# Cross-attention over 12,544 keys: values per tile, one matmul per head with high and low parts side by side, denominators on DVE, elementwise work in tiles of 1024 columns

## The reference

```python
lat = layernorm(latents, ln_l_w, ln_l_b)
ctx = layernorm(context, ln_c_w, ln_c_b)
q = (lat @ Wq).reshape(b, n, H, D).transpose(0, 2, 1, 3)
kv = ctx @ Wkv
k, v = jnp.split(kv, 2, axis=-1)
...
attn = jnp.einsum('bhnd,bhsd->bhns', q, k) * scale
attn = jnp.clip(attn, -11.0, 11.0)
attn = jax.nn.softmax(attn, axis=-1)
out = jnp.einsum('bhns,bhsd->bhnd', attn, v)
out = out.transpose(0, 2, 1, 3).reshape(b, n, INNER)
return out @ Wo + bo
```

## Time and profile before

| | us |
|---|---|
| median of three runs | 1161.74 (1159.35 to 1161.77) |
| profiled execution, its own time | 1157.79 |
| its span, first to last instruction | 1156.1 |
| PE busy | 1137.3 (98%) |
| DVE busy | 829.5 (72%) |
| ACT busy | 598.8 (52%) |
| POOL busy | 309.0 (27%) |

### The profile page before, as it was taken

How to read it: one execution, slowest core, us unless ns; L and a number is a source line. 1 busy time by engine, 2 the same in 40 slices (tenths; PEclk the granted TensorE clock), 3 DMA queues, 4 the chain that set the end, 5 groups by cost and what they waited for, 6 DMA issues and landing times.

```text
span 1156.1 us, 18331 instructions
## 1 busy us (share of the span) xinstructions
PE 1137.3 (98%) x5056; PEld 936.4 (81%) x5056; DVE 829.5 (72%) x1622; ACT 598.8 (52%) x1029; POOL 309.0 (27%) x516
## 2 busy tenths in 40 slices
PE   6999999999999999999999999999999999999997
PEld 5888888888888888888888888888888888888774
DVE  5778778777777777787776776776766766766624
ACT  4555555555555555555555555555555555555411
POOL 5334334334334233242221221221211211211100
PEclk8999999999999999999999999999999999999996
DMA  5221221221211211354212212212112112110000
GB/s 178 69 69 46 68 68 45 68 63 51 68 61 53 68 55 59 108 108 81 74 46 69 67 46 68 62 51 68 57 56 68 53 61 68 51 64 24 1 1 5
DMA packets 81393, 70.72 MB, mean 61 GB/s; under 512 B 40115, under 2 KB 67670, under 8 KB 81366
## 3 DMA queue, kind: packets, MB, share of 16 engines
q1 hardware_dynamic: 80390, 68.94, 20.1%
q10 hardware_dynamic: 976, 1.45, 0.4%
HBM read 70.13 MB, written 0.13 MB: 61 GB/s over the span
## 4 chain that ended last, share of the span: by engine, by line
PE 96%; issue 2%; DMA 1%; DVE 1%; POOL 0%; ACT 0%; SPq 0%; POOLq 0%; DVEq 0%; ACTq 0%
PE bank L466 31%; PE bank L467 31%; PE bank L468 31%; PE bank L511 1%; DMA wkT<-in_WkT_dram 1%; PE bank L572 1%; PE bank L584 1%; PE bank L503 0%; PE bank L614 0%; PE bank L596 0%; PE bank L630 0%; PE bank L594 0%; POOL wkT L457 0%; DVE fold_y L909 0%; PE bank L604 0%
## 5 line engine op out<-in xcount | busy, mean ns | idle before, releaser
L732 ACT ACTIVATE ex<-bank,c_rstd 128x512 f32<-128x512 f32 x392 | 270.1, 689 | 242.4 <-PE bank L468 166.4
L403 POOL TENSOR_TENSOR z_lo<-z,z_hi 128x255 fp32r<-128x255 f32 x196 | 174.9, 892 | 742.1 <-ACT z_hi L745 742.1
L739 ACT CAST p_hi<-ex 128x512 fp32r<-128x512 f32 x392 | 243.8, 622 | 240.8 <-DVE ex L899 148.6
L903 DVE TENSOR_TENSOR p_lo<-ex,p_hi 128x512 fp32r<-128x512 f32 x392 | 271.6, 693 | 116.3 <-ACT p_hi L739 99.7
L466 PE MATMUL bank<-qk_hi,d_hi 128*128 128x512 f32 x784 | 305.9, 390 | 0.0
L467 PE MATMUL bank<-qk_lo,d_hi 128*128 128x512 f32 x784 | 305.5, 390 | 0.0
L466 PE MATMUL bank<-p_hi,z_hi 128*128 128x512 f32 x784 | 305.5, 390 | 0.0
L468 PE MATMUL bank<-p_hi,z_lo 128*128 128x512 f32 x784 | 305.5, 390 | 0.0
L468 PE MATMUL bank<-qk_hi,d_lo 128*128 128x512 f32 x784 | 305.3, 389 | 0.0
L467 PE MATMUL bank<-p_lo,z_hi 128*128 128x512 f32 x784 | 305.2, 389 | 0.0
L899 DVE TENSOR_SCALAR ex<-ex 128x512 f32<-128x512 f32 x392 | 189.8, 484 | 156.5 <-ACT ex L732 154.6
(11 more groups left out here) (162 smaller groups left out, 410.0 us busy)
## 6 DMA issues: line engine op xcount, KB each, us to landing
t_all<-in_ctxT_dram SPq DMA_DIRECT2D x98, 384.0 KB, 3.2
x_pair<-in_ctx_dram SPq DMA_DIRECT2D x98, 256.0 KB, 2.7
diff<-sig_all SPq DMA_DIRECT2D x194, 0.5 KB, 1.9
wq<-in_Wq_dram ACTq DMA_DIRECT2D x2, 512.0 KB, 6.9
wkT<-in_WkT_dram SPq DMA_DIRECT2D x2, 512.0 KB, 6.1
wv<-in_Wv_dram SPq DMA_DIRECT2D x1, 1024.0 KB
wo<-in_Wo_dram SPq DMA_DIRECT2D x1, 1024.0 KB
crow_all<-in_crows_dram ACTq DMA_DIRECT2D x1, 256.0 KB, 7.6
```

The source lines that it names most:

```text
L403: pool.tensor_tensor(z_lo[s][:, b, 0:LAST], z[s][:, b, 0:LAST], z_hi[s][:, b, 0:LAST].bitcast(F32), ALU.subtract).then_inc(s_zlo, 1)
L732: act.activation(ex[c][:, :], sc_bank[c][:, :], ACT.Exp, scale=c_rstd[s4][:, b:b + 1])\
L739: act.copy(p_hi[b][c][:, :], ex[c][:, :]).then_inc(s_phi, 1)
L903: dve.tensor_tensor(p_lo[b][c][:, :], ex[c][:, :], p_hi[b][c][:, :].bitcast(F32), ALU.subtract)\
```

## The change

Three things change in the main loop. First, the values are made per tile: `values` multiplies the tile (`d_hi`, `d_lo`) with folded value weights `wv_hi`, `wv_lo` into one bank (128 keys x 512, 8 heads of 64), ACT and DVE split it into `vhl`, where each head's 64 high and 64 low columns lie side by side; z is gone, and with it POOL's part. Second, `weighted_sum` is one matmul per head: stationary `[v_hi | v_lo]` (128 columns), moving `[p_hi | p_lo]` of that head (256 columns). The four products land in four quarters of the result; the lo·lo one is summed too. `save_part` and `save` add the column halves; the halves on the partitions are added by a product with Wo stored twice (`wo2`). Third, the denominators are summed by DVE (`add_den`, 1024 columns per tile), added over the partitions by a matmul with ones, inverted 512 columns at a time (`inverse`) and multiplied in (`normalised`). The exponential stays in chunks of 512; clip, `p_hi` and `p_lo` take 1024 columns.

Around the loop: the weight folds for keys and values are matmuls with `foldT` (before the loop for pass 0, in the unrolled pairs for pass 1), Wo is applied for pass 0 inside pass 1's unrolled pairs, and ten matmuls on the identity stand at PE's start (`keep_warm`). The statistics of the rows are made in pass 0 only, as before; in pass 1 the rows themselves aren't loaded.

```diff
+            def values(p, gp, s, b, first=False):
+                g = 2 * gp + b
+                if b == 0:
+                    pe.wait_ge(s_dlo, gp + 1)
+                if not first:
+                    pe.wait_ge(s_vlo, g)
+                keys, cols = slice(b * P, (b + 1) * P), slice(p * IH, (p + 1) * IH)
+                for k in range(KD):
+                    ins = mm3(v_bank[:, :], d_hi[s][:, k, keys], d_lo[s][:, k, keys], wv_hi[:, k, cols], wv_lo[:, k, cols],
+                              k == 0, k == KD - 1)
+                ins.then_inc(s_v, 1)
...
-            def weighted_sum(gp, s, b, c, start, stop, saved=0):
+            def weighted_sum(gp, b, start, stop, saved=0):
                 g = 2 * gp + b
-                pe.wait_ge(s_plo, CH * g + c + 1)
-                if c == 0:
-                    pe.wait_ge(s_zlo, g + 1)
-                if saved:
-                    pe.wait_ge(s_save[c], saved)
+                pe.wait_ge(s_plo, g + 1)
+                pe.wait_ge(s_vlo, g + 1)
+                for m in range(MH):
+                    if saved:
+                        pe.wait_ge(s_save, saved - MH + m + 1)
+                    for a in range(2):
+                        at = m // CM * HC + a * CM + m % CM
+                        ins = pe.matmul(acc[m][:, a, :, :], vhl[b][:, 2 * m + a, :, :].rearrange("p n d -> p (n d)"),
+                                        ph[b][:, at, :, :], start=start and a == 0, stop=stop and a == 1)
+                ins.then_inc(s_pv, 1)
...
-                    ks = slice(k * P, (k + 1) * P)
-                    ins = mm3(acc[k][c][:, :], z_hi[s][:, b, ks], z_lo[s][:, b, ks], p_hi[b][c][:, :], p_lo[b][c][:, :],
-                              start, stop)
-                ins.then_inc(s_pv, 1)
...
+            def key_fold(half, ms, dst):
+                for n, m in enumerate(ms):
+                    for k in range(KD):
+                        ins = pe.matmul(dst[:, n * D:(n + 1) * D], wkv[:, 0, half, k, m * P:(m + 1) * P], foldT[:, k, :],
+                                        start=(k == 0), stop=(k == KD - 1))
...
+            keep_warm(10)
...
+            pe.wait_ge(s_wv[0], 16)
+            for k in range(KD):
+                value_fold(0, k, bank[k])
+            pe.wait_ge(s_wq[1], 16)
+            q_heads(1, range(MH), side_bank)
+            pe.wait_ge(s_wvlo, KD)
+            values(0, 0, 0, 0, first=True)
...
-                    for c in range(CH):
-                        if not ended:
+                    if next_p > p and not ended:
+                        pe.wait_ge(s_wvlo, KD * PASSES)
+                        pe.wait_ge(s_qklo, 2 * KD * CH)
+                    if not ended:
+                        values(next_p, gp + b, slot(p, phase, b, 2), 1 - b)
+                        for c in range(CH):
                             scores(next_p, gp + b, slot(p, phase, b, 2), 1 - b, c)
-                        weighted_sum(gp, slot(p, phase, 0, 2), b, c, first, last, saved=p * KD if first else 0)
...
+                    if p == 1 and extra in DEN_STEPS:
+                        denominators_0(extra)
...
+                pe.matmul(side_bank[:, :], ones_sq[:, :], den[0][:, c * HC:(c + 1) * HC, :], start=True, stop=True)\
+                  .then_inc(s_denp, 1)
...
+            def project(p, c, ats):
+                for at in ats:
+                    a, m = at // CM, c * CM + at % CM
+                    ins = pe.matmul(side_bank[:, 0:D], osum[p][c][:, a, m % CM, :], wo2[:, p * HP + 2 * m + a, :],
+                                    start=False, stop=(p == 1 and (c, at) == (CH - 1, HC - 1)))
...
+            pe.wait_ge(s_exp, CH * ALL)
+            pe.wait_ge(s_den, ALL)
+            for c in range(CH):
+                pe.matmul(DEN_BANK[c][:, :], ones_sq[:, :], den[1][:, c * HC:(c + 1) * HC, :], start=True, stop=True)\
+                  .then_inc(s_denp, 1)
             pe.wait_ge(s_lora, 1)
             effective_weights(1)
+            for c in range(CH):
+                pe.wait_ge(s_osn, CH + c + 1)
+                ins = project(1, c, range(HC))
+            ins.then_inc(s_xattn, 1)
...
+            def v_high(g, s4, b, used=True):
+                act.wait_ge(s_v, g + 1)
+                if used:
+                    act.wait_ge(s_pv, g - 1)
+                act.activation(vhl[b][:, :, 0, :], v_bank[:, :].rearrange("p (h d) -> p h d", h=HP), ACT.Identity,
+                               scale=c_rstd[s4][:, b:b + 1]).then_inc(s_vhi, 1)
...
+            def save_part(p):
+                act.wait_ge(s_pv, TILES * (p + 1))
+                for m in range(MH):
+                    act.copy(osum[p][m // CM][:, :, m % CM, :], acc[m][:, :, 0, :]).then_inc(s_part, 1)
...
+            def v_low(g, s4, b):
+                dve.wait_ge(s_vhi, g + 1)
+                dve.scalar_tensor_tensor(vhl[b][:, :, 1, :], v_bank[:, :].rearrange("p (h d) -> p h d", h=HP),
+                                         c_rstd[s4][:, b:b + 1], vhl[b][:, :, 0, :].bitcast(F32), ALU.mult, ALU.subtract)\
+                   .then_inc(s_vlo, 1)
...
+            def clip(g, b):
+                dve.wait_ge(s_exp, CH * g + CH)
+                dve.tensor_scalar(ex[b][:, :, :], ex[b][:, :, :], EXP_LO, EXP_HI, ALU.max, ALU.min).then_inc(s_clip, 1)
+            def p_low(g, b):
+                dve.wait_ge(s_phi, g + 1)
+                dve.tensor_tensor(ph[b][:, :, 1, :], ex[b][:, :, :], ph[b][:, :, 0, :].bitcast(F32), ALU.subtract)\
...
+            def add_den(p, g, b, first):
+                dve.wait_ge(s_clip, g + 1)
+                if first:
+                    dve.tensor_copy(den[p], ex[b][:, :, :]).then_inc(s_den, 1)
+                else:
+                    dve.wait_ge(s_den, g)
+                    dve.tensor_tensor(den[p], den[p], ex[b][:, :, :], ALU.add).then_inc(s_den, 1)
...
+                    if b == 0 and not (ended and i + 3 >= PAIRS):
+                        dve.wait_ge(s_tin[s3_4], landed(p, i, phase, 3, SLOTS))
+                        dve.wait_ge(s_dlo, gp + 2)
+                        difference(s3_4, s3)
+                    if b == 1 and not (ended and i + 2 >= PAIRS):
+                        d_low(gp + 2, slot(p, phase, 2, 2))
+                    add_den(p, g, b, first=static and i == 0 and b == 0)
+                    p_low(g, b)
+                    if b == 1 and more1:
+                        dve.wait_ge(s_crstd, stored(p, i, 1))
+                    if b == 1 and new_stats:
+                        dve.wait_ge(s_cst, 2 * gp + 8)
+                    if more1:
+                        v_low(g + 1, s4, 1 - b)
+                    if b == 0 and new_stats:
+                        ctx_stats(gp + 3, landed(p, i, phase, 3, SLOTS), s3_4, 0)
+                        ctx_stats(gp + 3, landed(p, i, phase, 3, SLOTS), s3_4, 1)
+                    if b == 1 and new_stats:
+                        ctx_aggr(s3, 0)
+                        ctx_aggr(s3, 1)
+                        ctx_veps(gp + 3, s3)
+                    if more1:
+                        clip(g + 1, 1 - b)
...
+                    if p == 1 and extra in DEN_STEPS:
+                        inverse(extra, side_bank)
+                        normalised(0, extra)
...
+            def save(p):
+                for m in range(MH):
+                    part = osum[p][m // CM][:, :, m % CM, :]
+                    dve.wait_ge(s_part, MH * p + m + 1)
+                    dve.tensor_tensor(part, part, acc[m][:, :, 1, :], ALU.add).then_inc(s_save, 1)
+            def inverse(n, src):
+                dve.wait_ge(s_denp, n + 1)
+                dve.reciprocal(rden[n % CH][:, :], src[:, :]).then_inc(s_rden, 1)
+            def normalised(p, c):
+                dve.wait_ge(s_rden, CH * p + c + 1)
+                dve.wait_ge(s_save, MH * p + CM * (c + 1))
+                flat = osum[p][c][:, :, :, :].rearrange("p a m q -> p (a m q)")
+                dve.tensor_tensor(flat, flat, rden[c][:, :], ALU.mult).then_inc(s_osn, 1)
...
+            for c in range(CH):
+                inverse(CH + c, DEN_BANK[c])
+            save(PASSES - 1)
+            for c in range(CH):
+                normalised(PASSES - 1, c)
```

More of the change, by code:

```diff
@@ L358, in pair @@
                         late(dst, src)
+                if static and p == 1 and i == 0:
+                    sp.wait_ge(s_wkEp, 2 * PASSES)
+                    sp.wait_ge(s_wvp, KD * PASSES)
+                    for half in range(2):
+                        sp.dma_start(wo2[half * DH:(half + 1) * DH, :, :], Wo).then_inc(s_wo, 16)
             assert (PAIRS - LOOPED - 1) * 3 >= len(late_loads)
@@ L516, in _, with keep_warm @@
+            def keep_warm(n):
+                for _ in range(n):
+                    pe.matmul(bank[6][:, 0:P], ident[:, :], ident[:, :], start=True, stop=True)
             pe.wait_ge(s_const, 1)
+            keep_warm(10)
             pe.wait_ge(s_latn, 1)
             for k in range(KD):
```

(40 more changed lines are left out.)

693 lines of the change are left out of this document (315 added, 378 removed).

## The result

The changed kernel took 1155.67 us (median of 13 runs, 1154.16 to 1160.86) against 1160.94 for the kernel before (13 runs), a ratio of 0.9962, 95% interval 0.9947 to 0.9976. The profiled execution has a span of 1154.8 us.

The account below looks back on a forecast made before the run. TensorE was taken to set the pace: loop -78.4, added matmuls +17.5, stalls +14, start -6.5, end -5, together -58.4 us on 1157.8, giving 1099.4. The forecast for the median was 1102 us, range 1074 to 1146.

Parts of the forecast that it names:

- the part on DVE: Main loop: whether DVE keeps up; 4.6 us a tile in pass 0, 4.1 in pass 1, against PE's 5.04.
- The chain named there: Inner loop, last score matmul to `p_lo`: 4.6 us under PE's 5.04, fits by 0.4, no stall counted.
- loses its subtraction altogether: Main loop, POOL: its subtraction goes, which also leaves DVE undisturbed; no separate size given.
- The matmul of 256 columns: Main loop on PE, fp32r: 120 ns each, between 107 (stream alone) and 188 (load not overlapping).
- The step: One tile on PE in the main loop: 5.04 us, 0.40 less than the 5.44 before.
- the loop's -78.4 us: Main loop on PE: 196 steps, each 0.40 us shorter.
- The weight load: Rival, main loop: fp32r loads don't overlap, 188 ns a matmul, 1208 us; chance 0.08 in full, 0.08 in part.
- rival 2: DVE sets pass 0's pace: 5.2 us a tile, 5.27 with the wait, +22 us, so 1124; chance 0.17.
- The inversions: DVE reciprocals of 512 columns: 3.3 us each; in pass 1 PE waits about 3 beside each, 6 together.
- The start: Ahead of the loop: first score at 17.5 us instead of 24.0, so -6.5, between 0 and -8.
- The end: After the last weighted sum, through the projection and norm: -5 us, between -8.6 and -3.
- the added matmuls and the stalls: Folds, denominators and Wo product on PE: +17.5 us; new waits at tiles, passes and inversions: +14 us.

Follow-up runs that it names:

- experiments 1 and 2: Experiment 1, and a second run: changed kernel with the pair's variances made on DVE one tile earlier, transfer still waiting for all three powers; 1104.37 us.
- experiment 4: Changed kernel with both edits, sigma transfer released two powers earlier and variances one tile earlier; 1104.96 us.
- experiment 8: Kernel of experiment 4 with DVE's `add_den` and `p_low` each cut into two halves of 512 columns; 1114.48 us.
- experiment 1: Changed kernel with SP issuing the sigma transfer after the first of POOL's three powers, not the third; 1105.15 us.

## Why the prediction was wrong

**The step that failed** is in the part on DVE: "It fits by 0.4 us. What is late next is this chain. In the inner loop I count no stall." The chain named there (exponential, clip, `difference`, `add_den`, `p_low`) does fit, by about as little as it says. But it isn't the only one. The change moves the variances to the end of the pair's second tile and lets `d_lo` for the same rows stand ahead of `add_den` in the next second tile, and between them lie POOL, SP, a transfer and ACT. That ring was never costed. The prediction even wrote that POOL "loses its subtraction altogether, which also leaves DVE undisturbed", and so looked at POOL as relief only. The ring cost 1155.67 - 1105 = 50.7 us of the 53.7 by which the forecast was missed, shown by experiments 1 and 2, from two sides.

Could it have been seen? The distance in program order, yes: 12.7 us between variances and `d_hi` before, 5.65 in the new order at PE's pace. The powers of the kernel before (groups of its loop: busy us, mean ns):

```profile
L390 POOL TENSOR_TENSOR sig_all<-c_veps,half_pow 128x2 f32 (+1 forms) x37 | 27.9, 755 | 23.1 <-DVE c_veps L879 23.1
L392 POOL TENSOR_TENSOR rstd_all<-c_veps,neg_half 128x2 f32 (+1 forms) x37 | 27.9, 754 | 0.0
L391 POOL TENSOR_TENSOR c_rstd<-c_veps,neg_half 128x2 f32<-128x2 f32 x37 | 25.3, 684 | 0.0
```

With these durations the path is 0.35 to POOL's start, 2.2 for the powers, 0.14 to the issue of the first half of the transfer, 0.65 to the second's, 1.91 until that has landed and 0.1 to `d_hi`: 5.35 together, which would just have fitted into 5.65, with so little to spare that a stall belonged among the bounds. What made it 7.02 is that the powers now meet 1024-column instructions and take 3.87, 1.67 more. Both halves of the change's wording are in it, "denominators by DVE" and "whole tiles of 1024 columns".

**The other terms.**
- The matmul of 256 columns: forecast 120 ns; eight of them take 303.08 to 304.03, 0.95 us, 119 ns each. The step: 5.04 forecast, 5.06 in pass 1. Of the loop's -78.4 us, 74.5 was earned (196 x 0.38), and 50.7 was given back. The forecast took 226.7 ns for the six matmuls of the values too, whose spacing is 232 (1.39 us behind 304.03). The weight load, the rival that I gave for slower, doesn't decide at 119. The Trainium skill's "TensorE: Matmul & The Clock Gate" (Back-to-back issue gap) gives 109 for it; the trace says 119, 16 us more over 1568 matmuls.
- DVE's throughput (rival 2, 1124): net of overlaps 4.6 us a tile were forecast; in experiment 4 DVE is busy 404.8 us of 440 in the loop of pass 0, 87 tiles, so 4.66, and doesn't pace PE there. It is close to it: experiment 8 shows the loss that 0.28 us per pair more brings. The spacing of 1024-column neighbours is 1.13 at a duration of 1.22, so the overlap of 0.08 holds at this size too.
- The inversions: forecast 3.3 us each, measured 3.29.

```profile
1103.09 6.57 DVE L1101 RECIPROCAL rden<-wide 128x512 f32<-128x512 f32 x2 [3.88 <-PE wide L663]
```

  The slope over 15 columns carried to 512. The Trainium skill's "VectorE: DVE Perf Modes" (the 8-slice pipeline in each mode) has the divide step repeated 8 times. My estimate from it, 8 times an ordinary op's column and 4.5 us, is refuted by this row. The two waits beside the inversions in pass 1 are 2.94 each, forecast about 3.
- The start: first score at 17.5 forecast, 15.36 measured, so -8.7 instead of -6.5, just outside my range of 0 to -8.

```profile
15.36 0.47 PE L455 MATMUL wide<-qk_hi,d_hi 128*128 128x512 f32 x1
```

- The end: 3.1 us forecast for the last tile's wait, 2.96 measured; from the last weighted sum to the span's end 53.7, where it was 61.2: -7.5 instead of -5. The projection with Wo came after a standstill of 4.1 us, in the stretch whose granted clock is 0.72 in the mean, and took 347 ns a record.

```profile
1099.27 2.08 PE L494 MATMUL wide<-ph,vhl 128*128 128x256 f32 x8 [2.96 <-DVE ph L967]
...
1111.58 5.55 PE L641 MATMUL wide<-wkv,osum 128*128 128x256 f32 x16 [4.10 <-DVE osum L1107]
```

Taken together the terms that I did write down were right within 4 us: the sum says -58.4 on the profiled execution, and with the ring opened (experiment 1) the spans differ by 54.3 (1156.1 and 1101.8). In part they offset each other. The step gave 3.9 less than forecast, start and end in that kernel 3.9 more (its first score is at 16.43, its last part 53.4), and 35.6 is left, by subtraction, for the added matmuls and the stalls, forecast at 31.5. That 1105 lies only 3 from 1102 is a little luck, for the kernel before came out 2 us lower in later runs as well. The sum was good; what was missing was a path.

## What to carry to other kernels

When a change moves an instruction on one engine, list every value that goes out from there and comes back (here DVE, POOL, SP, transfer, ACT, DVE) and compare the path's length with the time that the new order leaves for it, even where the engines on it are 20% busy: a ring's period, not a share, is its bound. A small instruction of POOL that reads SBUF cost its own time plus the rest of the two-input DVE instruction, or of the clip, that it met, so longer DVE instructions lengthened POOL's path even as they saved DVE time. And a semaphore that counts several results should be waited for at the one that is needed.
